# The tail of a fused four-layer kernel: routing from small matmuls of its own, gate products on GpSimd, banks and turns given out anew

## The reference, cut to what matters

```python
x = x + _L0_xattn_ref(...)      # a WKV scan over 256 steps
x = x + _L0_ffn_ref(...)        # quantised matmul
x = x + _L1_xattn_ref(...)      # 16 heads of self and cross attention, and a projection
x = x + _L1_ffn_ref(_layernorm(x), ...)   # the tail

# _L1_ffn_ref: 4 positions l, 16 heads of 8 (q, k) and 16 (v)
x = silu(x_prev * conv_w[:, 0] + x * conv_w[:, 1])
q = silu(x @ Wq); k = x @ Wk; v = x @ Wv; g = x @ Wg
q = _apply_rotary(q, cos, sin); k = _apply_rotary(k, cos, sin)
logits = einsum('bhld,hdr->bhlr', v, router_w)          # 2 routes
scores = softmax(logits); onehot = one_hot(argmax(scores), 2)
sum_ind = cumsum(onehot, axis=2)
norm = where(sum_ind > 0, 1.0 / maximum(sum_ind, 1.0), 0.0)[..., None]
q_exp = q[..., None, :] * (scores * onehot)[..., None] * norm
k_exp = k[..., None, :] * onehot[..., None]
qk = einsum('bhld,bhmd->bhlm', q_exp, k_exp) * HDK ** (-0.5) * tril(ones)
o = einsum('bhlm,bhmd->bhld', qk, v)
o = (o - mean(o)) / sqrt(var(o) + EPS)                  # over each head
out = (silu(g) * o) @ Wout
```

## Time and profile before

| | us |
|---|---|
| three runs: median (lowest to highest) | 672.46 (672.37 to 672.68) |
| the profiled execution: its own time | 672.11 |
| its span in the trace | 670.3 |
| PE busy | 612.7 (91%) |
| DVE busy | 531.5 (79%) |
| ACT busy | 398.0 (59%) |
| POOL busy | 256.2 (38%) |

### The profile page before, as it was taken

The page is one execution under the profiler, slowest core; times in us unless marked ns, Lnnn a source line. Parts: engine busy times, 40 slices in busy tenths (PEclk is TensorE's granted clock), DMA queues, the critical chain, the costliest instruction groups (busy, mean ns, idle before and its releaser), DMA issues.

```text
span 670.3 us, 13297 instructions
## 1 busy us (share of the span) xinstructions
PE 612.7 (91%) x4567; PEld 490.7 (73%) x4567; DVE 531.5 (79%) x1305; ACT 398.0 (59%) x1339; POOL 256.2 (38%) x338
## 2 busy tenths in 40 slices
PE   4446999999999999999999999999999999999936
PEld 3345787777778787777788877877888888877725
DVE  7998687988887778888777788888664677868697
ACT  4255766666877545667566456575663665554531
POOL 2115664444333544343344443333332444430233
PEclk9997999999999999999999999999999999999978
DMA  8237452442592202322343232232353234020001
GB/s 266 88 151 200 169 166 56 126 156 89 180 334 100 96 22 102 104 103 106 104 124 99 92 103 103 104 104 103 103 168 100 103 103 103 17 33 1 1 0 63
DMA packets 36973, 72.86 MB, mean 109 GB/s; under 512 B 3343, under 2 KB 28587, under 8 KB 32811
## 3 DMA queue, kind: packets, MB, share of 16 engines
q1 hardware_dynamic: 36720, 72.00, 33.4%
q10 hardware_dynamic: 186, 0.02, 0.0%
HBM read 59.41 MB, written 12.60 MB: 107 GB/s over the span
## 4 chain that ended last, share of the span: by engine, by line
PE 63%; DVE 20%; issue 7%; POOL 5%; ACT 4%; DMA 0%; DVEq 0%; POOLq 0%
PE bank L722 13%; PE bank L702 11%; PE bank L591 10%; PE bank L598 6%; PE bank L674 5%; PE bank L746 3%; PE bank L688 3%; PE bank L703 3%; POOL rs L1343 2%; ACT square L1087 2%; DVE nm L1760 2%; DVE Cb L1775 2%; PE bank L832 2%; PE bank L736 1%; PE bank L841 1%
## 5 line engine op out<-in xcount | busy, mean ns | idle before, releaser
L722 PEld LDWEIGHTS bank<-V,Pt 128*128 128x128 f32 x1024 | 128.1, 191 | 28.7 <-DVE Cb L1775 14.9
L1087 ACT ACTIVATE square<-bank 128x128 bf16<-128x128 f32 x372 | 97.9, 280 | 83.8 <-PE bank L591 70.2
L722 PE MATMUL bank<-V,Pt 128*128 128x129 f32 x1024 | 136.3, 276 | 3.0 <-DVE Cb L1775 2.8
L702 PE MATMUL bank<-QT,KTt 128*128 128x512 f32 x256 | 132.6, 599 | 2.2 <-POOL diag L1358 2.2
L1358 POOL TENSOR_TENSOR diag<-identb,nm 128x512 bf16<-128x512 bf16 x64 | 66.9, 1045 | 174.0 <-DVE nm L1760 173.9
L1070 ACT ACTIVATE Pt<-bank 128x512 f32<-128x512 f32 x128 | 76.9, 601 | 64.1 <-PE bank L703 60.9
L1760 DVE TENSOR_REDUCE nm<-bank 128x2 f32<-128x512 f32 x128 | 82.4, 685 | 27.0 <-PE bank L688 26.6
L1343 POOL TENSOR_TENSOR rs<-ve,mhalf 128x6 f32<-128x6 f32 x64 | 90.0, 1406 | 5.3
L1775 DVE SCALAR_TENSOR_TENSOR Cb<-bank,ro,ism 128x128 bf16<-128x128 f32 x256 | 78.1, 347 | 4.5
L591 PE MATMUL bank<-WQ,xq 128*128 128x256 f32 x512 | 79.3, 297 | 1.0 <-DVE xq L1671 1.0
L1087 ACT ACTIVATION_READ_ACCUMULATOR square<-bank 128x1 f32 x372 | 78.1, 210 | 0.0
(11 more groups left out here) (233 smaller groups left out, 1019.8 us busy)
## 6 DMA issues: line engine op xcount, KB each, us to landing
WQ<-wq_split SPq DMA_DIRECT2D x24, 1024.0 KB, 7.8
WH<-wh_split SPq DMA_DIRECT2D x24, 384.0 KB, 8.9
wq_split<-WQ SPq DMA_DIRECT2D x8, 1024.0 KB, 4.5
ism<-smooth_inverse SPq DMA_DIRECT2D x32, 256.0 KB, 6.4
wst<-in_L_xattn_wproj SPq DMA_DIRECT2D x16, 256.0 KB, 4.5
wh_split<-WH SPq DMA_DIRECT2D x8, 384.0 KB, 3.2
wst<-in_L_xattn_wq SPq DMA_DIRECT2D x8, 256.0 KB, 4.6
wst<-in_L_xattn_wqx SPq DMA_DIRECT2D x8, 256.0 KB, 4.8
```

What stands on the lines that cost most here:

```text
L702: nc.tensor.matmul(o[:], KTt[u % 2][:, x, t * P:(t + 1) * P], QT[u % 2][:, x, :], start=True, stop=False)
L722: last = nc.tensor.matmul(o[:, h * (P + 2):h * (P + 2) + P + 1], Pt[:, x, k, h * S + t * P:h * S + (t + 1) * P], V[u % 2][:, x, k, 0:P + 1 ...
L1087: last = A(square[:, t, h], head(t, h), ACT.Square, accum_out=ss[:, t, h:h + 1])
```

## The change

1. **Routing** is taken out of the projections. `route_logits` computes it with matmuls of 16 columns into bank XB: positions 0 to 2 at once between the two tiles of position 0, position 3 inside the second tile of position 1. ACT's tanh reads the bank; DVE's `route3(0, 3)` and `route3(3, 4)` compute signs, magnitudes, pair masks, counts and finished pair weights `wt`. `dots3` is left with three operations: product, sum, times `wt`.
2. **Gate products** `weigh3` of positions 0 to 2 move from DVE to POOL, between the rotations. POOL rotates tile by tile (`rotate3(l, t)`, six operations of 64 elements).
3. **Convolution**: ACT's `turned3` writes the scaled input into `cv` directly (position 0 with silu at once), so DVE has one operation for each half instead of two.
4. **Order and banks**: 12 of the 64 matmuls of `project_last` go into unit 30, `turn_inputs3` goes between the `weigh` steps of unit 31, the rest of `project_last` goes around `turn_outputs(31)`; the residual of tile 0 no longer waits for tile 1; banks are dealt out so that these fit.
5. `variance3(l)` follows `mix3(l)` directly for positions 0 to 2.

```diff
+            def project_last(t, groups):
+                pe.wait_ge(s["catT_evac"], UNITS - G + groups[-1] + 1)
+                if t and groups[0] == 0:
+                    pe.wait_ge(s["qt_evac"], 4 * UNITS)
+                for g in groups:
+                    for f in (x * HEADS + g * HPG + h for x in range(2) for h in range(HPG)):
...
+            def route_logits(l0, l1):
+                free(XB)
+                pe.wait_ge(s["silu_ready"], l1)
+                for l in range(l0, l1):
+                    for t in range(NT):
+                        for k in range(KT):
+                            o = (l * NT + t) * H3
+                            last = nc.tensor.matmul(XB[:, o:o + H3], cv[:, k, l, t * P:(t + 1) * P], W3[:, k, R0:R0 + H3],
+                                                    start=k == 0, stop=k == KT - 1)
+                last.then_inc(s["route_done"], 1)
...
@@ PE, units 30 and 31
                 weigh(u, 1, 1)
+                if u == UNITS - 2:
+                    project_last(0, (0,))
...
                 guard(u + 1, 1)
+                if u == UNITS - 2:
+                    project_last(0, (1, 2))
...
             weigh(u, 0, 1)
+            turn_inputs3(0)
             weigh(u, 1, 0)
+            turn_inputs3(1)
             weigh(u, 1, 1)
-            for l in range(B - 1):
-                turn_inputs3(l)
-            project_last(0, True)
+            turn_inputs3(2)
+            project_last(0, (3, 4, 5, 6))
+            project_last(1, (0, 1, 2, 3))
             turn_outputs(u)
-            project_last(1, True)
-            project_last(0, False)
-            project_last(1, False)
-            project3(0)
+            project_last(1, (4, 5, 6))
+            project_last(0, (7,))
+            project_last(1, (7,))
+            project3(0, 0)
+            route_logits(0, B - 1)
+            project3(0, 1)
             turn_inputs3(B - 1)
-            for l in range(1, B):
-                project3(l)
+            project3(1, 0)
+            project3_keys(1, 1)
+            route_logits(B - 1, B)
+            project3_gate(1, 1)
...
@@ ACT
+                for c in range(KT):
+                    last = A(cv[:, c, l, :], x[:, c], ACT.Copy if l else ACT.Silu, scale=vc(f"conv{c}", 1))
...
             projected3(0)
+            route3(0, B - 1)
             projected3(1)
             turned3(B - 1)
-            route3(0)
+            silu3(B - 1)
             projected3(2)
+            route3(B - 1, B)
+            squares3(0)
             projected3(3)
-            squares3(0)
...
@@ POOL
+            def weigh3(l):
+                pool.wait_ge(s["sq_ready"], l + 1)
+                gp.tensor_tensor(rows3(g3, l), rows3(g3, l), rows3(o3, l), ALU.mult).then_inc(s["og_ready"], 1)
...
-            for l in range(1, B):
-                rotate3(l)
+            rotate3(1, 0)
+            weigh3(0)
+            rotate3(1, 1)
+            rotate3(2, 0)
+            rotate3(2, 1)
+            weigh3(1)
+            rotate3(3, 0)
+            rotate3(3, 1)
+            weigh3(2)
             for l in range(B - 1):
                 gate3(l)
...
@@ DVE
+            def route3(l0, l1):
+                n = 1 if l0 == 0 else 2
+                dve.wait_ge(s["th_done"], n)
+                d = XB[:, l0 * n3:l1 * n3].rearrange("p (l n) -> p l n", n=n3)
+                c = cf[:, l0:l1]
+                v.tensor_scalar(sel[:, l0:l1], d, 0.0, None, ALU.is_ge).then_inc(s["dl_ready"], 1)
+                ch.add(v.scalar_tensor_tensor(out=c, in0=c, scalar=-1.0, in1=c, op0=ALU.mult, op1=ALU.max))
+                dve.wait_ge(s["dl_ready"], n)
+                ls = [l for l in range(l0, l1) if l]
+                for l in ls:
+                    ch.add(v.tensor_tensor(route_weights(l), sel[:, 0:l + 1], sel[:, l:l + 1].to_broadcast([P, l + 1, n3]),
+                                           ALU.is_equal))
...
             def dots3(l):
...
-                link(v.tensor_tensor(same[:, 0:m, :], sel[:, 0:m, :], sel[:, l:l + 1, :].to_broadcast([P, m, n3]), ALU.is_equal))
...
-                link(v.tensor_reduce(cnt[:], same[:, 0:m, :].rearrange("p m n -> p n m"), AX_X, ALU.add))
                 if l == B - 1:
                     head_rstd3()
-                dve.wait_ge(s["th_done"], l + 1)
-                ch.add(v.reciprocal(cnt[:], cnt[:]))
-                ch.add(v.tensor_scalar(cf[:, l], cf[:, l], 0.5, 0.5, ALU.mult, ALU.add))
-                link(v.tensor_tensor(lm[:, 0:m, :], lm[:, 0:m, :], same[:, 0:m, :], ALU.mult))
...
-                link(v.tensor_tensor(lm[:, 0:m, :], lm[:, 0:m, :], cnt[:].unsqueeze(1).to_broadcast([P, m, n3]), ALU.mult))
+                link(v.tensor_tensor(lm[:, 0:m, :], lm[:, 0:m, :], route_weights(l) if l else cf[:, 0:1], ALU.mult))
...
-            route3(0)
+            route3(0, B - 1)
             dots3(0)
+            convolve3(B - 1)
             mix3(0)
-            convolve3(B - 1)
-            route3(1)
-            weigh3(0)
             variance3(0)
...
+            route3(B - 1, B)
+            for l in range(1, B):
+                dots3(l)
+                mix3(l)
+                if l == B - 1:
+                    weigh3(l)
+                variance3(l)
```

More of the change, by code:

```diff
@@ L180, in build_program @@
         lm = lb("lm", [P, B, NT * H3])
-        same = lb("same", [P, B, NT * H3])
-        cnt = lb("cnt", [P, NT * H3])
+        cnt = lb("cnt", [P, 2, NT * H3])
         m3 = lb("m3", [P, B, NT * H3])
@@ L276, in high, with route_weights @@
             return turned[:, x, :].bitcast(BF16).rearrange("p (n e) -> p n e", e=2)[:, :, 1]
+        def route_weights(l):
+            o = l * (l + 1) // 2
+            return wt[:, o:o + l + 1, :]
         def rows3(buffer, l):
@@ new lines, in project3_keys @@
+                if m >= 2:
+                    pe.wait_ge(s["qkv3_evac"], 3 * (m - 2) + 2)
+                o = P3A[m % 2]
+                for k in range(KT):
+                    last = nc.tensor.matmul(o[:, 0:G0], cv[:, k, l, t * P:(t + 1) * P], W3[:, k, 0:G0], start=k == 0,
+                                            stop=k == KT - 1)
+                for k in range(KT):
+                    last = nc.tensor.matmul(o[:, G0:2 * D], cv[:, k, l, t * P:(t + 1) * P], wk[:, k], start=k == 0,
+                                            stop=k == KT - 1)
@@ new lines, in project3_keys, with project3_gate, project3 @@
+                last.then_inc(s["proj3_done"], 1)
+            def project3_gate(l, t):
+                m = l * NT + t
+                if m >= 2:
+                    pe.wait_ge(s["qkv3_evac"], 3 * (m - 2) + 3)
+                for k in range(KT):
+                    last = nc.tensor.matmul(P3B[m % 2][:, 0:D], cv[:, k, l, t * P:(t + 1) * P], W3[:, k, G0:R0], start=k == 0,
+                                            stop=k == KT - 1)
+                last.then_inc(s["proj3_done"], 1)
+            def project3(l, t):
+                project3_keys(l, t)
+                project3_gate(l, t)
@@ L1873, in convolve3 @@
                 for c in range(KT):
-                    now, before = vc(f"conv{c}", 1), vc(f"conv{c}", 0)
                     o = cv[:, c, l, :]
-                    last = v.tensor_scalar(o, hT[:, c, l, :], now, None, ALU.mult)
-                    if l:
-                        link(last)
-                        last = v.scalar_tensor_tensor(out=o, in0=hT[:, c, l - 1, :], scalar=before, in1=o, op0=ALU.mult,
-                                                      op1=ALU.add)
+                    last = v.scalar_tensor_tensor(out=o, in0=hT[:, c, l - 1, :], scalar=vc(f"conv{c}", 0), in1=o, op0=ALU.mult,
+                                                  op1=ALU.add)
                     if c < KT - 1:
@@ L1956, in weigh3 @@
                 dve.wait_ge(s["sq_ready"], l + 1)
-                last = v.tensor_tensor(rows3(g3, l), rows3(g3, l), rows3(o3, l), ALU.mult)
-                if l < B - 1:
-                    last.then_inc(s["og_ready"], 1)
-                else:
-                    ch.add(last)
+                dve.wait_ge(s["qkv3_evac"], 3 * T8)
+                ch.add(v.tensor_tensor(rows3(g3, l), rows3(g3, l), rows3(o3, l), ALU.mult))
             def finish3(l):
```

151 lines of the change are left out of this document (62 added, 89 removed).

## The result

| | before | after |
|---|---|---|
| median of 20 runs (lowest to highest), us | 672.25 (672.08 to 672.89) | 673.61 (672.37 to 675.47) |
| ratio of the runs, 95% interval | | 1.0017 [1.0011, 1.0024] |
| the profiled execution / its span | 672.11 / 670.3 | 673.87 / 672.1 |

The changed kernel is slower by 0.17% (1.1 us by the ratio, 1.4 by the medians). The forecast was 672.4, practically no change, so the time fell within the stated range, but the kernel moved the other way than forecast. Its runs also lie further apart than those of before.

The account below looks back on a forecast made before the run. The tail was bound by PE to about 620.6, DVE from about 633 to its reciprocal at 653.51, then the end part. Reciprocal -2.3 and end +2.2 gave 672.46 - 0.1 = 672.4 us, range 669.6 to 674.2.

Parts of the forecast that it names:

- project3 starts: First tail projection on PE: 618.5 instead of 620.6, by moving output-projection matmuls and input turning earlier.
- thin matmuls: New 16-column routing matmuls on PE: 0.107 per record, 24 records 2.57 and 8 records 0.86.
- wait for the squares of 1 and 2: DVE before variances 1 and 2: with gate products removed, it waits 0.7 each for ACT's squares.
- R: End of DVE's 128x96 reciprocal, which releases POOL's first final product: 651.2, 2.3 earlier than 653.51.
- PE's projections end: PE's last output projection after DVE's 128x96 reciprocal: R + 13.7 against R + 11.47, 2.2 longer.
- without that cover up to 0.8 each: POOL's gate products in the tail: cost if DVE's waits and one-input sums did not cover them.
- POOL gets the ports first: Rival, end of tail: POOL's first final product issues ahead of DVE's 2048-element product; 671.3, chance 0.20.
- The lag of 0.5: Time from the reciprocal's end to POOL's first final product; put DVE's product at R + 0.98, ahead of R + 1.26.
- the clock's return: PE's granted clock in the end part: back to 1.00 at R + 8.4, 4.1 after PE's restart.
- The 2.83 of the earlier trace: PE's output projection of position 0 at the end, taken as 2.83 at half clock.
- -2.3 + 2.2: Forecast's sum: 128x96 reciprocal 2.3 earlier, end part after it 2.2 longer, giving -0.1.
- colliding gate products: Case on POOL and DVE in the tail: three port collisions at 0.8, 674.8; chance 0.13 together with exposed weight loads.

Follow-up runs that it names:

- first experiment: Kernel before with only the parts that let PE reach the tail sooner, old routing, gate products and dots: 670.14 us, 0.9969.
- the woven kernel: Changed kernel with the 16-column matmuls of positions 0 to 2 placed in pairs between wide matmuls of position 0's first tile: 672.77 us, 1.0013.
- three edits: Changed kernel with gate products on DVE, 128x96 reciprocal ahead of position 3's sum, position 0's squares ahead of position 3's tanh: 667.68 us, 0.9929.
- reciprocal ahead of the sum: Changed kernel with DVE's 128x96 reciprocal placed ahead of the sum of position 3's dots: 669.77 us, 0.9970.
- scale in the square root: Changed kernel with the variance's small scale-and-add folded from DVE into ACT's square root: 672.91 us, 1.0003.
- squares first: Changed kernel with ACT taking position 0's squares before position 3's tanh: 671.60 us, 0.9991.

## Why the prediction was wrong, step by step

Times of after on before's clock.

| step | predicted | measured |
|---|---|---|
| project3 starts | 618.5 | 618.44 |
| thin matmuls | 2.57 + 0.86 | 2.60 + 0.81 |
| variance 0 | 632.85 | 632.84, after 3.45 idle, ended by ACT |
| dots 1 / end of position 1's mix | 635.7 / 639.65 | 635.88 / 639.62 |
| wait for the squares of 1 and 2 | 0.7 each | 0.70, 0.69 |
| dots 2 | 641.15 | 642.18 |
| R | 651.2 | 652.47 |
| PE's projections end | R + 13.7 | R + 13.83 |

**Right:** what bounds what. The early projection is worth its 2.1 (first experiment), a thin record costs as much as one of 128 columns (0.108 against 0.11), as the weight load that the prediction took for it would have it, and variance 0 is late because PE's thin matmuls, ACT's tanh and the squares stand in one line. Up to the mix of position 1 no step is off by more than 0.2. That a removed gate product uncovers the squares held too.

**The step that failed** is "POOL's gate products (1.07 each) fall into DVE's waits and one-input sums, so I cost them at nothing". The collision came at an operation with one input, the scale-and-add of 32 elements: 1.22 and 0.97 for 0.18, 1.83 in all. The sentence behind it, "without that cover up to 0.8 each", was the right size for the wrong condition. POOL was late for DVE's wait (its second gate product began at 641.45, 0.64 after the wait had ended), because DVE's own large products had stretched the rotations in front (four operations from 638.32 took 2.45 for 1.04). Of these 1.83, 0.57 came back, since contention in position 2 was less than assumed: R is 1.27 later than predicted. The experiment on the gate products shows this directly: with them on DVE the operations take 0.18 to 0.31 again and R comes 1.55 earlier.

**The end had the right size by luck: two errors cancelled.** In the profiled execution the rival "POOL gets the ports first" happened: first final product at R + 0.83, 0.10 ahead of the large product, which then took 3.10; the first was done at 654.85, 1.06 after its start (the prediction had named 1.07 as a sign of being wrong); the second was done at R + 5.0 (predicted R + 4.9). The lag of 0.5 on which I put the large product ahead was not repeated: it was 0.08 here, and 0.23 with the gate products on DVE. That rival's end was R + 12.0 to 13.1, and the woven kernel shows it: R + 12.81. In the changed kernel's own profile the clock came back 8.3 after PE's restart instead of 6.2, and that makes R + 13.83.

The second error is the clock's return, which the prediction put 4.1 after the restart from a single row. Where its own order of products came about (gate products on DVE), the clock returned 7.3 after the restart and the end was R + 15.09 for R + 13.7. The 4.1 came from an execution without a pause between the turnings. Over all traces, without a pause the clock returned 3.7 to 6.0 after the restart (six kernels), and with the pause of 1.93 after 6.2 to 8.3 (seven); counted from the end of the pause that is 3.2 to 5.2. This fits the condition that the prediction gave only as a bound, that the pause starts the wait anew, but no run varied the pause alone, and the spread of some 2 within each set is unexplained. The 2.83 of the earlier trace rows that the prediction calls work at half clock ran in part at full clock; wholly at half clock it takes 3.57 (656.43 to 660.00 with the projection ahead of the turning). This reading left the forecast's sum as it is.

**Why slower:** predicted -2.3 + 2.2; measured -1.04 + 2.36, and the 1.27 between the first terms is the gate products on POOL. The case "colliding gate products" had its place in the sum of chances for slower (0.13 with another), but was priced at three collisions, 2.4 in all; there were two, of 0.8 and 1.0. The 1.3 that is left of them puts the forecast at 673.7, just under the 673.8 from which the prediction called the kernel slower.

**Open:** what parts the changed kernel's runs. They run from 672.4 to 675.5, some 1.2 between two clusters (six of 672.4 to 673.0, nine of 673.6 to 673.9). A late return of the clock costs 1.0 in one trace, the fall behind the thin block 1.67 in two others, and who is first at the ports lies within 0.10; each could do it. The mean granted clocks of the twenty runs speak for the clock: the ten runs with 0.982, the profiled one among them, all take 673.2 or more, and the slowest has 0.977, while of the six lowest one has 0.985 and five 0.962 or 0.964. But one run of 0.985 and two of 0.962 lie in the upper cluster too, and of the changed kernel's other runs there is no trace.

## What to carry to other kernels

Before an operation is moved off an engine, look up what wait it covered there, and at what the other engine's instruction will meet when it is late: not only two-operand instructions, but small one-operand ones too. If a result is awaited elsewhere with two-operand work, release it ahead of a long one-operand reduction and not ahead of a large product; moving one reciprocal in this way gave 3.8 on the changed kernel, where POOL's second product had waited for the large one, and 0.9 on the old routing, where it had not. A matmul with few columns costs as much as one of 128 columns here. Spreading a row of them among wide ones took the upper group of runs away in two kernels at a price of about 0.3, and brought nothing in the best one.

## What was not expected of the hardware

- A one-input TENSOR_SCALAR (f32, 32 elements a partition, in place) of DVE is held back by POOL's product to that product's end: 1.22 and 0.97 for 0.18. TENSOR_REDUCE is not: 0.69 with and without POOL beside it. The Trainium skill (SBUF — State Buffer, Who interferes with whom) says so: `tensor_scalar` can take the shared ports, `tensor_reduce` on trn2 cannot. The prediction had used that section only for two-input work.
- POOL's gate product takes 1.26 even with DVE idle, against 0.69 on DVE.
- The granted clock fell while PE was busy throughout: 3 us at 0.50 behind 24 records of 16 columns, in the profiled executions with the block at 620.61 and 620.75, not in four others with it at 621.01 to 621.29 nor in the changed kernel's at 621.53, and not in the one with 12 records at 620.60.
- The clock's return after PE's restart, in the profiled executions. Without a pause between the two turnings: 4.2 (before), 3.7 (early projection alone), 4.8 (old routing, reciprocal moved), 4.9 and 4.6 (three edits, without and with weaving), 6.0 (reciprocal ahead of the sum). With the pause of 1.93: 8.3 (the changed kernel), 7.2 (scale in the square root), 8.0 (squares first), 6.2 (half of the thin matmuls), and 6.2, 7.6 and 8.2 (woven, alone and with these two edits). With a shorter pause: 7.3 with 0.86 (gate products on DVE), 6.4 with 0.69 (projection ahead of the turning). The Trainium skill (TensorE: Matmul & The Clock Gate, What's actually happening) says that the number of matmuls at the low clock varies between runs of one kernel. The woven and the changed kernel, 6.2 and 8.3 with the same work and the same pause, would fit that, but they are two kernels with one trace each.
